# Attention with a feed-forward branch on one core: half-batch pipeline, with the transposes of O moved from TensorE to VectorE

## The reference

```python
xn = layernorm(x)                            # x: (16, 256, 256) float32, eps 1e-5
qkv = xn @ w_qkv                             # 16 heads of 16
scores = (q / 4) @ k.T, causal               # per head, 256 x 256
attn_out = softmax(scores) @ v @ w_out
g, u = fp8(xn) @ fp8(w_gating[0]), fp8(xn) @ fp8(w_gating[1])    # 256 -> 1024
ffn_out = fp8(gelu(g) * u) @ fp8(w_linear)
out = x + attn_out + ffn_out
```

## Time and profile before

| what | value |
|---|---|
| three runs | 408.47, 412.04 (median), 413.58 us |
| the profiled execution | 413.38 us, its span 411.6 us |
| attention stage, steady steps | from 171.55 to 350.41 us of the span, eleven equal steps |
| PE, DVE, ACT, POOL busy over the span | 90%, 72%, 54%, 26% |

### The profile page before, as it was taken

How to read it: one execution, slowest core, us unless ns; L and a number is a source line. 1 busy time by engine, 2 the same in 40 slices (tenths; PEclk the granted TensorE clock), 3 DMA queues, 4 the chain that set the end, 5 groups by cost and what they waited for, 6 DMA issues and landing times.

```text
span 411.6 us, 9925 instructions
## 1 busy us (share of the span) xinstructions
PE 370.4 (90%) x3658; PEld 277.6 (67%) x3658; DVE 297.6 (72%) x1324; ACT 222.9 (54%) x320; POOL 108.7 (26%) x140
## 2 busy tenths in 40 slices
PE   7699899987898889999999999999999999889774
PEld 7255345555556767878878778788787787666543
DVE  5878878893565678878888788788787887886112
ACT  1775676654552165565555665655656556555540
POOL 2230433303102023223222332322232323233320
PEclk9999999999999699999999999999999999998875
DMA  7974764535361345064263362551642622300000
GB/s 242 352 264 116 203 195 128 128 120 179 130 229 62 137 164 200 35 208 171 63 232 116 120 213 80 174 181 57 230 148 87 232 94 90 104 29 2 29 25 25
DMA packets 46519, 57.58 MB, mean 140 GB/s; under 512 B 2632, under 2 KB 39048, under 8 KB 46472
## 3 DMA queue, kind: packets, MB, share of 16 engines
q1 hardware_dynamic: 46472, 56.96, 42.0%
HBM read 16.78 MB, written 12.58 MB: 71 GB/s over the span
## 4 chain that ended last, share of the span: by engine, by line
PE 75%; DVE 9%; ACT 7%; issue 4%; DMA 2%; POOL 1%; SPq 0%; DVEq 0%; POOLq 0%; ACTq 0%
PE ps L742 12%; PE ps L667 11%; PE ps L721 9%; PE ps L655 7%; PE ps L773 7%; PE ps L703 6%; PE ps L674 5%; PE ps L628 4%; PE ps L635 4%; PE ps L758 4%; DVE act L393 3%; PE ps L765 2%; ACT w_raw L550 2%; DVE masked L428 2%; PE ps L604 2%
## 5 line engine op out<-in xcount | busy, mean ns | idle before, releaser
L428 DVE CUSTOM_DVE_ANT_0 masked<-ps,causal 128x256 bf16<-128x256 f32 (+1 forms) x512 | 149.2, 350 | 36.9 <-PE ps L703 36.9
L557 ACT ACTIVATE arena<-ps 128x1024 f32<-128x1024 f32 x96 | 98.7, 1028 | 76.9 <-PE ps L721 76.6
L315 POOL TENSOR_SCALAR_AFFINE_SELECT arena<-arena 128x512 f32<-128x512 f32 (+1 forms) x96 | 75.7, 789 | 193.2 <-ACT arena L557 193.2
L721 PE MATMUL ps<-stack 64*128 64x256 f32 (+1 forms) x512 | 51.7, 301 | 5.2 <-ACT arena L557 3.9
L667 PE MATMUL ps<-xs,wq_part 128*128 128x256 f32 x384 | 54.8, 294 | 1.5 <-DVE wq_part L384 0.7
L742 PE MATMUL ps<-arena,v_aug 128*32 128x256 f32 (+1 forms) x1024 | 54.7, 345 | 1.0 <-POOL arena L315 1.0
L393 DVE TENSOR_TENSOR act<-ps,gate 128x512 fp8e4<-128x512 f32 x64 | 43.1, 685 | 16.2 <-ACT gate L506 14.5
L703 PE MATMUL ps<-stack 63*128 63x256 f32 (+1 forms) x512 | 49.4, 292 | 5.4 <-DVE row_max L428 4.9
L667 PEld LDWEIGHTS ps<-xs,wq_part 128*128 128x128 f32 x384 | 49.3, 196 | 2.8 <-ACT ffn L530 1.2
L506 ACT ACTIVATE gate<-ps 128x512 bf16<-128x512 f32 x64 | 38.0, 599 | 17.7 <-PE ps L628 11.3
L721 PEld LDWEIGHTS ps<-stack 64*128 64x128 f32 x512 | 36.5, 189 | 15.7 <-ACT arena L557 8.1
(11 more groups left out here) (54 smaller groups left out, 361.7 us busy)
## 6 DMA issues: line engine op xcount, KB each, us to landing
stack<-qk_part SPq DMA_DIRECT2D x96, 256.0 KB, 2.6
xt_store<-xt_part SPq DMA_DIRECT2D x16, 512.0 KB, 4.5
xs<-xt_store SPq DMA_DIRECT2D x16, 512.0 KB, 3.9
out_dram<-w_raw SPq DMA_DIRECT2D x16, 256.0 KB, 2.8
xres<-in_L_attn_x_dram SPq DMA_DIRECT2D x7, 512.0 KB, 6.5
arena<-in_L_ffn_w_gating_dram SPq DMA_DIRECT2D x2, 1024.0 KB, 9.3
stack<-zeros SPq DMA_DIRECT2D x4, 512.0 KB, 7.6
arena<-in_L_ffn_w_linear_dram SPq DMA_DIRECT2D x1, 1024.0 KB, 13.2
```

Of the source, the lines that this page charges most:

```text
L315: nc.gpsimd.affine_select(diag, diag, pattern=[[0, 1024 // width], [1, P]], compare_op=ALU.is_ge, fill=0.0, base=0, channel_multiplier=-1) ...
L428: last = nc.vector.tensor_tensor_reduce(masked[:, place, i * width:(i + 1) * width], max_ps[:, place, i * width:(i + 1) * width], causal[: ...
L557: nc.scalar.activation(arena[:, n, :, :], exp_ps, ACT.Exp).then_inc(exp_done, 1)
L721: last = nc.tensor.matmul(exp_ps[:, u, i * width:(i + 1) * width], st[rows, j0 + i, 1, kt * P:(kt + 1) * P], st[rows, j0 + i, 0, kt * P:S] ...
```

## The change

Q, K and V are made as before. What differs:

- **Halves of batches.** Heads 0 to 7 and 8 to 15 now go through maxima, exponentials, V, normalization and output as two halves c. The maxima are transposed, negated and placed twice a batch (8 rows each), and `times_v` runs twice (32 matmuls each) in place of four times 16. Steps overlap differently: the exponentials of a batch all stand in one step, and its output comes two steps behind them.
- **O.** DVE turns O straight from PSUM in blocks of 32x32 (`o_to_rows`, 128x512), divides in SBUF and turns each half back by a second block transpose (128x256). The 12 PE transposes and `save_o` are gone. ACT rounds from SBUF, and POOL subtracts (`split_ot`).
- **Q and K.** ACT copies them raw to SBUF, DVE rounds them to the high part by a cast from SBUF to SBUF, POOL subtracts (`split_qk`).
- **Maxima** are negated by ACT. **Output**: ACT copies it from PSUM and POOL adds the residual, both work that one DVE instruction did.

```diff
@@ SP, in the loop over s @@
+            def place_max(b, c):
+                sp.wait_ge(neg_done[c], b + 1)
+                sp.dma_start(stack[b % NB][ROW:P:64, 4 * c:4 * c + 4, 0, :].bitcast(F32),
+                             neg_max[c][:, :].bitcast(F32)).then_inc(neg_in[c], 16)
...
@@ POOL @@
+            def split_qk(b, g):
+                pool.wait_ge(qk_hi[g], b + 1)
+                nc.gpsimd.tensor_tensor(qk_part[:, g, QLO:KLO + 1:3, :], qk_raw[:, g, :, :], qk_part[:, g, QHI:KLO, :].bitcast(F32),
+                                        ALU.subtract).then_inc(qk_lo[g], 1)
...
+            def split_ot(b, c):
+                pool.wait_ge(ot_hi, 2 * b + c + 1)
+                nc.gpsimd.tensor_tensor(ot_part[:, 1, c, :], ot_raw[:, c, :], ot_part[:, 0, c, :].bitcast(F32),
+                                        ALU.subtract).then_inc(ot_lo, 1)
+
+            def add_x(b):
+                pool.wait_ge(y_copied, b + 1)
+                nc.gpsimd.tensor_tensor(y[b % 2][:, :, :], y[b % 2][:, :, :], xres[:, b * QT:(b + 1) * QT, :], ALU.add).then_inc(y_done, 1)
+
+            for s in range(B + 5):
+                if has(s - 2):
+                    mask(s - 2, 5)
+                if has(s - 3):
+                    split_ot(s - 3, 1)
+                if s >= 1 and has(s + 1):
+                    split_qk(s + 1, 0)
+                if has(s - 1):
+                    mask(s - 1, 1)
+                    mask(s - 1, 2)
+                if has(s - 4):
+                    add_x(s - 4)
+                if s >= 1 and has(s + 1):
+                    split_qk(s + 1, 1)
+                if has(s - 1):
+                    mask(s - 1, 3)
+                    mask(s - 1, 4)
+                if has(s - 2):
+                    split_ot(s - 2, 0)
+                if has(s):
+                    mask(s, 0)
...
@@ DVE @@
+            def round_qk(b, g):
+                dve.wait_ge(qk_copied[g], b + 1)
+                if b >= 1:
+                    dve.wait_ge(stacked[g], 48 * b)
+                nc.vector.tensor_copy(qk_part[:, g, QHI:KLO, :], qk_raw[:, g, :, :]).then_inc(qk_hi[g], 1)
...
+            def o_to_rows(b, c):
+
+                dve.wait_ge(pv_ready, 2 * b + c + 1)
+                nc.vector.transpose(o_by_q, pv_ps).then_inc(o_by_q_done, 1)
+
+            def normalize_o(b, c):
+                done = 2 * b + c + 1
+                o = o_by_q.rearrange("p (k e) -> p k e", e=2 * DH)
+                dve.wait_ge(o_by_q_done, done)
+                nc.vector.reciprocal(r_den[:, :], o[:, :, DH]).then_inc(den_done, 1)
+                dve.wait_ge(den_done, done)
+                nc.vector.tensor_tensor(o_norm[:, :].rearrange("p (k u d) -> p u k d", u=2, d=DH),
...
+                nc.vector.transpose(ot_raw[:, c, :], o_norm[:, :]).then_inc(ot_ready, 1)
...
@@ ACT @@
+            def copy_qk(b, g):
+                act.wait_ge(qk_ready[g], b + 1)
...
+                nc.scalar.copy(qk_raw[:, g, :, :], misc[:, 1, :].rearrange("p (a s) -> p a s", a=2)).then_inc(qk_copied[g], 1)
...
+                nc.scalar.mul(neg_max[c][:, :], misc[0:PAIRS, 1 - c, 0:S], -1.0).then_inc(neg_done[c], 1)
...
+                nc.scalar.copy(ot_part[:, 0, c, :], ot_raw[:, c, :]).then_inc(ot_hi, 1)
+
+            def copy_y(b):
+                act.wait_ge(ot_used, 2 * b + 2)
...
+                nc.scalar.copy(y[b % 2][:, :, :], misc[:, 0, :].rearrange("p (t d) -> p t d", t=QT)).then_inc(y_copied, 1)
...
@@ PE @@
-            def transpose_o(b):
...
-            def transpose_back(b):
...
+            def transpose_max(b, c):
+                pe.wait_ge(max_done, 2 * UNITS * b + UNITS * (c + 1))
...
+            def project_out(b, c):
+                pe.wait_ge(ot_lo, 2 * b + c + 1)
...
+                if has(s - 1):
+
+                    pe.wait_ge(*((y_copied, s - 3) if s >= 4 else (v_done, s + 1)))
+                    transpose_max(s - 1, 1)
                 if s >= 1 and has(s + 1):
 
+                    pe.wait_ge(qk_copied[0], s + 2)
                     project_qk(s + 1, 1)
```

More of the change, by code:

```diff
@@ L44, in attention_ffn @@
     HG = 4
-    G = H // HG
     PAIRS = H // 2
@@ L465, in _ @@
+            for s in range(B + 3):
                 if has(s - 1):
@@ L761, in transpose_back @@
[L761 to L775 removed]
+                if 2 * b + c >= 1:
+                    pe.wait_ge(o_by_q_done, 2 * b + c)
@@ new lines, in times_v @@
+                for u in range(2):
+                    for kt in range(QT):
+                        for i in range(HG):
+                            if kt == 0:
+                                cols = arena[:, 3 * c + 1 + i // 2, u, i % 2 * S:(i % 2 + 1) * S]
+                            else:
+                                cols = arena[:, 3 * c, u, i * P:(i + 1) * P]
+                            last = nc.tensor.matmul(pv_ps[32 * i:32 * i + 32, u * S + kt * P:(u + 1) * S],
+                                                    va[:, kt, 2 * (HG * c + i) + u, :], cols,
+                                                    start=(kt == 0), stop=(kt == QT - 1), tile_position=(0, 32 * i),
+                                                    skip_group_check=True)
@@ L779, in _ @@
                 if has(s - 1):
-                    max_scores(s - 1, 4)
-                if has(s - 2):
-                    times_v(s - 2, 0)
-                if has(s - 3):
-                    transpose_back(s - 3)
-                if s >= 1 and has(s + 1):
-                    pe.wait_ge(*((o_norm_done, s - 2) if s >= 3 else (v_done, s + 1)))
-                    project_qk(s + 1, 1)
-                if has(s - 2):
-                    exp_scores(s - 2, 3)
-                if has(s - 1):
-                    max_scores(s - 1, 5)
-                if has(s - 2):
-                    times_v(s - 2, 1)
-                if has(s - 3):
-                    project_out(s - 3)
-                if has(s - 2):
-                    exp_scores(s - 2, 4)
+                    exp_scores(s - 1, 0)
                 if has(s):
@@ L811, in _ @@
+                    transpose_max(s - 1, 1)
+                if s >= 1 and has(s + 1):
+                    pe.wait_ge(qk_copied[0], s + 2)
+                    project_qk(s + 1, 1)
                 if has(s):
                     max_scores(s, 1)
+                if has(s - 1):
+                    exp_scores(s - 1, 1)
                 if has(s + 1):
-                    pe.wait_ge(*((neg_done, s) if s >= 1 else (ffn_done, 2 * CHUNKS - 1)))
+                    pe.wait_ge(*((neg_done[1], s) if s >= 1 else (ffn_done, 2 * CHUNKS - 1)))
@@ new lines, in _ @@
+                    transpose_max(s, 0)
+                if has(s - 3):
+                    pe.wait_ge(*((v_done, s + 2) if has(s + 1) else (neg_done[1], s) if has(s - 1) else (y_copied, s - 3)))
+                    project_out(s - 3, 0)
+                if has(s - 1):
+                    exp_scores(s - 1, 4)
+                if has(s):
+                    max_scores(s, 4)
+                if has(s - 3):
+                    project_out(s - 3, 1)
+                if has(s + 2):
+                    pe.wait_ge(neg_done[0], s + 1)
+                    project_qk(s + 2, 0)
@@ L841 @@
+                if has(s - 1):
+                    exp_scores(s - 1, 5)
+                if has(s):
+                    max_scores(s, 5)
+                if has(s - 1):
+                    times_v(s - 1, 0)
 _INS = ["L0_attn_x", "L0_attn_w_qkv", "L0_attn_w_out", "L0_ffn_w_gating", "L0_ffn_w_linear"]
```

271 lines of the change are left out of this document (109 added, 162 removed).

## The result

The changed kernel takes 390.22 us (median of 4 runs, 388.51 to 394.47), the kernel before 410.83 us (median of 4, 408.47 to 413.58). The ratio is 0.948, with a 95% interval from 0.939 to 0.957: **faster by 5%**. The run of 394.47 us, more than 1.5% above the fastest, is not in the ratio. The profiled execution's span is 387.9 us, 23.7 less than 411.6. The medians differ by 20.6 us; the profiled execution before was the slowest of its four.

A forecast was written before the change was run, and what follows sets the result against it. The prediction took PE to set the old step of 16.26 us, and DVE's work with its waits the new one of 15.35. 413.4 - 11.8 (steps) - 9.6 (end) = 392.0 us, forecast 384 to 399, range 382 to 408.

The forecast's parts named there:

- PE's floor: PE's own list allows a step of 14.43 us; as a rival, reached, 380 us, chance 0.12 for under 384.
- DVE's own work: DVE's operations in a step: 9.0 us of maxima remain and 4.43 us come, 13.45 us in all.
- The waits for POOL: DVE's SBUF casts and multiplications wait for POOL operations on a shared port pair, 1.1 us a step.
- The wait for ACT's copy: DVE, after maxima unit 5, waits 0.6 us for ACT's raw copy of Q and K before casting.
- PE's hole: PE waits 0.7 us a step for DVE's maxima, ahead of `max_scores` unit 4.
- DVE's floor is the bound: DVE's summed work of 13.45 us, plus waits and hand-overs, sets the step.
- The walk: Timeline of one new step across the engines, from PE finishing `max_scores` unit 5, closing at 15.35 us.
- The number of steps: Thirteen full steps (s = 2 to 14) gain 0.91 us each, 11.8 us; the others gain nothing.
- The end: From the last transposition of maxima to the kernel's end: 22.0 us in place of 31.6, 9.6 less.
- Transposes in two or four passes: Rivals on DVE's block transposes: two passes, 413 us, within chance 0.18 for 404 to 420; four, 454 us, chance 0.06.
- Waits at every SBUF operation: Rival: DVE waits for POOL eight times a step, not four; 406 us, within chance 0.18 for 404 to 420.
- SP: SP's transfer of the half batch's row of maxima has over a microsecond of room.

The follow-up runs named there:

- e4: Changed kernel with DVE's casts of Q and K gone, ACT making the high part by a second copy from PSUM: 378.42 us, ratio 0.920, step 14.31 us.
- e3: Changed kernel with POOL's addition of x behind the second subtraction of Q and K, SP's output store behind placing the maxima: 376.57 us, ratio 0.915.
- e8: e4's kernel with e1's added matmuls: span 381.0 us against 371.7, step 14.79 us, 0.48 more.
- e2: Changed kernel with a second, unread reciprocal on DVE in each half batch: span 388.9 us, step 15.59 us.
- e5: Changed kernel with one DVE fill a step right ahead of the second cast of Q and K: span 389.0 us, step 15.58 us.
- e6: Changed kernel with one DVE fill a step right behind the second cast of Q and K: span 389.0 us, step 15.80 us.
- e7: Changed kernel with its part on Q and K undone (ACT rounds and DVE subtracts from PSUM, no POOL): 390.11 us, ratio 0.949, step 15.25 us.
- e1: Changed kernel with unit 4's four matmul pairs of the exponential's scores issued three times over: span 387.8 us, step 15.59 us.

## Why the prediction was right, point by point

- **PE's floor** (14.43 us): right. e4 reaches 14.31 us, e3 14.51, and e8 shows that in e4 PE's list sets the step.
- **DVE's own work** (13.45 us): right within 0.35 us. DVE is busy 14.99 us of a step, and without the 1.89 us of waits for POOL that is 13.10. The open price, the block transpose from PSUM, came out at 710 ns (0.69 taken; 0.43 and 1.22 were the bounds), the one from SBUF at 446 (0.42 taken), the reciprocal at 245 (0.26). The pace is (710 - 446)/256, 1.03 ns an element, and the prediction's ordinary operation has 1.04. The Trainium skill, "Vector Engine (DVE) Microarchitecture Reference", section 3.8, has one element a cycle and lane for the transpose; the trace agrees in so far as there is no second pass.
- **The waits for POOL** (1.1 us): the mechanism was right, the size too small, 1.89 us. The term that failed is the cast's: I had it behind a mask for 0.5 us, but POOL was earlier than walked and had just begun the addition of x: 1.04 us.
- **The wait for ACT's copy** (0.6 us) was 0.32, half. With 0.79 us too little for POOL, 0.28 too much for ACT and 0.35 too much for DVE's own work, three errors nearly cancel, and that is luck: the step came to 15.58 and not 15.35, and PE's hole to 1.0 and not 0.7.
- **"DVE's floor is the bound"**, as a sum: this reading fell with e2 and e5. The walk had it right, since it ended waits by POOL's clock; the sum beside it did not say which DVE work counts.
- **The number of steps** (13 steps x 0.91 = 11.8 us) gave the right total, 12.1, by a wrong division. Ten steady steps gained only 0.68 us each, 6.8 in all. The three ahead of them gained 6.6 us. In two of those the output's matmuls, 1.6 us, had not begun after the change, and in the second they had begun before it; in the first the kernel before ran at the low clock for 3.7 us. Only the third (1.8 us) is short for want of the addition on POOL that delays the cast. The last two lost 1.4 us, and the 16.33 us in it are 2.2 us more than e2, e5 and e6 took there with less of the low clock. The steps I gave nothing, ahead of the first mark, gained 2.5 us, some 1.4 of it by the low clock before (2.76 against 1.67 us in one `project_qk`, and 0.3 us in the matmuls ahead of it). The runs' first marks spread from 137.2 to 139.4 us besides (e7's and e8's left out), so a gain of the change is not shown there.
- **The end** (22.0 us behind the last transposition, 9.6 less): measured 22.5 and 9.1. About 3 us of the 9.1 are the clock again. Before, it was at 0.50 from 396.2 us on, and the last `times_v`, both transposes and `project_out` took 3.2 us more than at 1.00 a little earlier (`project_out` 2.93 against 1.70 us). After, the last matmuls ran at 1.00, where the forecast had priced them at the low clock. One stretch of 3.3 to 3.5 us at 0.50, some microseconds behind the last mark, stands in both.
- **The whole**: the sum started from the profiled 413.4 us, the slowest run before. The gain of 21.4 us that it forecast stands beside 20.6 between the medians and 23.7 between the profiled spans.
- **The rivals**: PE's floor was not reached by the change but was one edit of POOL's order away (376.57 us; 380 was worked out for it). Transposes in two or four passes did not occur. Waits at every SBUF operation didn't either: three of DVE's eight in a step waited.
- **SP** had the room that the forecast gave it: no wait for it in ten steps of the changed kernel, one of 0.51 us in e1.
- What the forecast did not see at all is that the part on Q and K costs 0.33 us a steady step in this order and shows no gain in the whole (e7).

## What to carry to other kernels

Where one engine's SBUF operations hold up another's, place the long ones by the timeline, not by what is ready: a POOL addition ahead of the subtraction that waits for DVE's cast cost 13.6 us (390.22 to 376.57, with SP's store moved too), with no work added or removed; 10.7 of them stand in the ten steady steps. Before pricing an engine by its sum of work, ask for each piece whether a wait with another engine's time as its end follows; work ahead of such a wait was free here, behind it was paid. And to find a term of under 0.3 us a step, read the distance between steady steps, since spans differ by more. Read the granted clock of each stretch before you give its difference to the change: here the steady steps compared at 1.00, and the stretches around them did not.

## What the runs showed of the hardware that was not expected

- A fill of 512 bf16 elements on DVE was issued as 256 elements of 4 bytes and took 0.27 us (e5).
- ACT's copy from SBUF took 401 ns for 256 contiguous elements (L605), against 517 in the earlier trace rows for the one that rearranges; no run separates the pattern from the stage.
- A DVE operation that POOL holds up ends 0.27 to 0.29 us behind POOL's, whether it is a cast of 0.43 us or a multiplication of 0.42, and whether POOL adds, subtracts or, for the cast, fills. Its own time is not added in full to what was left of POOL's.
- POOL is held too: its subtraction of Q and K, 1.27 to 1.28 us alone, took 1.47 us in each step where DVE's multiplication had started ahead of it, and 1367 ns on average.
